# Single-unit places for the side work in the second and the last batch of a selective scan

## The reference, cut to what matters

```python
x = einsum('ed,bld->bel', in_proj_w, hidden)            # DI = 512 channels
u = silu(conv4(x) + conv_b)
x_dbl = einsum('ke,bel->bkl', x_proj_w, u)               # dt_lo (16), B (16), C (16)
delta = softplus(dt_proj_w @ dt_lo + dt_proj_b)
state = state * exp(delta * A) + (delta * u) * B         # over 512 steps, 16 states n
y = sum_n state * C + D * u
x = x + tanh(g_x) * (y * silu(layernorm(x)))
x = x + tanh(g_f) * moe(layernorm(x))                    # top 6 of 16 experts and a shared one
```

## Time and profile before

| what | us |
|---|---|
| three runs, median | 1437.23 (1434.22 to 1439.29) |
| profiled execution, its own time | 1440.73 |
| its span in the trace | 1438.6 |
| batch 0, first scan to first scan of batch 1 | 46.3 to 159.2 |
| batch 1 (second) | 159.2 to 273.4, 114.2 |
| batch 2 (third) | 273.4 to 385.1, 111.7 |
| batch 3 (last) | 385.1 to 488.2, 103.1 |
| last product of POOL in the scans | ends at 491.67 |
| experts | from 492.4 to the end |

### The profile page before, as it was taken

One profiled execution on the slowest core, in us unless ns is written; L12 is line 12 of the kernel. 1 busy time (PEld: TensorE's weight loads), 2 busy tenths in 40 slices (PEclk: granted clock), 3 DMA queues, 4 the chain that ended last, 5 costly groups with the idle time before them and its releaser, 6 DMA issues.

```text
span 1438.6 us, 32257 instructions
## 1 busy us (share of the span) xinstructions
PE 1355.8 (94%) x8480; PEld 1212.9 (84%) x8481; DVE 786.1 (55%) x1362; ACT 730.9 (51%) x1317; POOL 952.3 (66%) x673
## 2 busy tenths in 40 slices
PE   7897998998898899999999999999999999999996
PEld 2686887887888799999998989989889888898895
DVE  5878898898999854653333333333333333333331
ACT  5898897898889464343332333323333233333321
POOL 0588899998998847887455665556645666646631
PEclk8899999998999999999999999999999999999998
DMA  4121123222242365645455435555445544455332
GB/s 137 38 68 37 53 67 96 67 85 79 75 157 68 124 130 105 143 83 140 83 143 144 130 64 142 143 144 135 113 84 141 144 131 108 97 137 138 75 60 36
DMA packets 65042, 149.13 MB, mean 104 GB/s; under 512 B 16976, under 2 KB 17616, under 8 KB 62656
## 3 DMA queue, kind: packets, MB, share of 16 engines
q0 software_dynamic: 31024, 62.10, 22.7%
q1 hardware_dynamic: 33392, 81.21, 17.2%
q10 hardware_dynamic: 560, 4.98, 1.0%
HBM read 101.50 MB, written 48.99 MB: 105 GB/s over the span
## 4 chain that ended last, share of the span: by engine, by line
PE 65%; ACT 2%; DVE 2%; issue 1%; POOL 0%; DVEq 0%; POOLq 0%; ACTq 0%
PE bank L1706 20%; PE bank L1686 19%; PE bank L1687 18%; PE bank L1674 3%; PE bank L1697 3%; DVE hs L1168 1%; PE bank L1591 1%; ACT dA L784 1%; PE bank L1577 1%; PE bank L1589 0%; ACT gt L799 0%; POOL hc L945 0%; DVE xl L1359 0%; DVE du L1182 0%; ACT bdiag L802 0%
## 5 line engine op out<-in xcount | busy, mean ns | idle before, releaser
L945 POOL TENSOR_TENSOR hc<-hs,crow 128x512 f32<-128x512 f32 x256 | 325.0, 1304 | 91.7 <-DVE hs L1168 86.2
L1686 PE MATMUL bank<-w,xh 128*128 (+1 forms) x1088 | 368.9, 340 | 8.1 <-issue 4.7
L1011 POOL DMA_INDIRECT out_x<-ys,aid x104 | 170.7, 1641 | 277.0 <-issue 218.8
L1687 PE MATMUL bank<-w,xh 128*128 (+1 forms) x1088 | 351.0, 323 | 0.0
L1168 DVE TENSOR_TENSOR_SCAN hs<-dA,bank 128x512 f32<-128x512 f32 x256 | 295.8, 1208 | 48.5 <-PE bank L1591 31.8
L1706 PE MATMUL bank<-w,ah 128*128 (+1 forms) x816 | 266.0, 407 | 2.7 <-DVE al L1395 2.7
L1395 DVE TENSOR_TENSOR al<-bank,ah 128x384 fp32r<-128x384 f32 x136 | 75.9, 558 | 331.6 <-ACT ah L860 280.4
L1686 PEld LDWEIGHTS bank<-w,xh 128*128 128x128 f32 x1088 | 204.3, 188 | 37.8 <-issue 34.8
L1687 PEld LDWEIGHTS bank<-w,xh 128*128 128x128 f32 x1088 | 206.3, 190 | 2.2
L866 ACT COPY ys<-bank 128x512 f32<-128x512 f32 x136 | 79.9, 587 | 196.7 <-PE bank L1706 189.0
L1687 PE MATMUL bank<-w,xl 128*128 (+1 forms) x544 | 175.8, 323 | 0.0
(11 more groups left out here) (183 smaller groups left out, 2056.6 us busy)
## 6 DMA issues: line engine op xcount, KB each, us to landing
wraw<-in_wall SPq DMA_DIRECT2D x16, 2176.0 KB
crow<-c_rows SPq DMA_DIRECT2D x64, 256.0 KB, 3.3
xt<-token_rows_turned SPq DMA_DIRECT2D x32, 256.0 KB
out_x<-ys POOLq DMA_DIRECT2D x32, 256.0 KB
wraw<-in_wall ACTq DMA_DIRECT2D x2, 2176.0 KB
token_rows<-rowb SPq DMA_DIRECT2D x4, 1028.0 KB
xrow<-in_x SPq DMA_DIRECT2D x4, 1024.0 KB, 8.0
out_x<-xrow SPq DMA_DIRECT2D x4, 1024.0 KB, 4.9
```

The lines of the kernel that those rows point to most:

```text
L945: nc.gpsimd.tensor_tensor(hc[:, j, :], hs[:, j, :], crow[:, n % 4, :], ALU.mult).then_inc(hc_done, 1)
L1011: pool.indirect_dma_start(out_rows, bass.IndirectOffsetOnAxis(ap=aid[:, s:s + 1], axis=0), ys[:, s, :], None, bounds_check=TOKENS - 1, oob ...
L1686: nc.tensor.matmul(gate_bank[:, 0:I], xx, columns(w, off + ww + k * 2 * I, I), start=first, stop=last)
L1687: mm = nc.tensor.matmul(up_bank[:, 0:I], xx, columns(w, off + ww + k * 2 * I + I, I), start=first, stop=last)
```

## The change

It changes tables only: every piece stays on its engine and in its batch, and the same set of pieces is done. In batch 1 and batch 3 they now stand behind other units, mostly singly; the tables of batches 0 and 2 are as before. Two entries change their order within ACT's list: in batch 1 `table` now stands before `silu` and `siluz`, and in batch 3 `siluz` stands behind unit 40 and `table` behind unit 45. SP's pieces (loads and stores) of these batches move too, and POOL's `low` pieces of the last batch.

```diff
-PE_SECOND = {3: [("xproj", "pre", 0), ("xproj2", "pre", 0)], 7: [("dt", "pre", 0), ("dt", "pre", 1)], 11: [("dt", "pre", 2)], 15: [("dt", "pre", 3)],
-             23: [("bt", "pre", 0)], 27: [("inproj", "next", 0)], 35: [("xlt", "epi", 0), ("inproj", "next", 1), ("xlt", "epi", 1)],
-             39: [("inproj", "next", 2), ("xlt", "epi", 2)], 43: [("inproj", "next", 3)], 47: [("xlt", "epi", 3)],
-             51: [("gate", "epi", 0), ("dut", "pre", 0), ("gate2", "epi", 0), ("dut", "pre", 1)], 55: [("szt", "own", 0), ("dut", "pre", 2)],
-             59: [("szt", "own", 1), ("szt", "own", 2), ("dut", "pre", 3), ("szt", "own", 3)]}
+PE_SECOND = {3: [("xproj", "pre", 0), ("xproj2", "pre", 0)], 8: [("dt", "pre", 0)], 9: [("dt", "pre", 1)], 14: [("dt", "pre", 2)],
+             17: [("dt", "pre", 3)], 25: [("bt", "pre", 0)], 27: [("inproj", "next", 0)],
+             35: [("xlt", "epi", 0), ("inproj", "next", 1), ("inproj", "next", 2)], 36: [("xlt", "epi", 1)], 40: [("xlt", "epi", 2)],
+             43: [("inproj", "next", 3)], 47: [("xlt", "epi", 3)], 51: [("gate", "epi", 0), ("gate2", "epi", 0), ("dut", "pre", 0)],
+             53: [("dut", "pre", 1)], 55: [("szt", "own", 0), ("dut", "pre", 2)], 59: [("szt", "own", 1)], 60: [("szt", "own", 2)],
+             61: [("szt", "own", 3), ("dut", "pre", 3)]}
...
-ACT_SECOND = {11: [("xproj", "pre", 0)], 15: [("decay", "pre", 0)], 19: [("decay", "pre", 1)], 23: [("decay", "pre", 2), ("softplus", "pre", 0)],
...
-              43: [("xlt", "epi", 1), ("inproj", "next", 2)], 47: [("inproj", "next", 3), ("xlt", "epi", 2)],
-              51: [("xlt", "epi", 3), ("silu", "next", 0), ("siluz", "own", 0), ("table", "own", 0)], 55: [("dut", "pre", 0), ("dut", "pre", 1)],
-              59: [("dut", "pre", 2), ("szt", "own", 0)],
-              63: [("szt", "own", 1), ("szt", "own", 2), ("szt", "own", 3), ("dut", "pre", 3), ("gate", "epi", 0)]}
...
+              33: [("softplus", "pre", 2)], 35: [("softplus", "pre", 3), ("rstd", "both", 0)], 36: [("norm", "epi", 0)],
+              39: [("xlt", "epi", 0), ("inproj", "next", 1)], 40: [("inproj", "next", 2)], 41: [("xlt", "epi", 1)], 47: [("xlt", "epi", 2)],
+              49: [("inproj", "next", 3)], 52: [("xlt", "epi", 3), ("table", "own", 0), ("silu", "next", 0), ("siluz", "own", 0)],
+              55: [("dut", "pre", 0)], 58: [("dut", "pre", 1)], 59: [("gate", "epi", 0)], 62: [("szt", "own", 0), ("dut", "pre", 2), ("szt", "own", 1)],
+              63: [("szt", "own", 2), ("szt", "own", 3), ("dut", "pre", 3)]}
...
-ACT_LAST = {19: [("rstd", "both", 0)], 23: [("norm", "epi", 0)], 26: [("high", "last", 0)], 27: [("xlt", "epi", 0), ("xlt", "epi", 1)],
-            28: [("high", "last", 1)], 30: [("high", "last", 2)], 32: [("high", "last", 3)], 34: [("high", "last", 4)], 36: [("high", "last", 5)],
-            38: [("high", "last", 6)], 39: [("xlt", "epi", 2), ("xlt", "epi", 3)], 40: [("high", "last", 7)],
-            43: [("siluz", "own", 0), ("table", "own", 0), ("szt", "own", 0)], 47: [("szt", "own", 1)], 55: [("szt", "own", 2)],
-            59: [("szt", "own", 3), ("gate", "epi", 0)]}
+ACT_LAST = {22: [("rstd", "both", 0), ("norm", "epi", 0)], 24: [("high", "last", 0), ("high", "last", 1)], 27: [("xlt", "epi", 0)],
+            29: [("xlt", "epi", 1)], 30: [("high", "last", 2)], 34: [("high", "last", 3)], 35: [("high", "last", 4)], 38: [("high", "last", 5)],
+            39: [("high", "last", 6), ("xlt", "epi", 2), ("xlt", "epi", 3)], 40: [("siluz", "own", 0)], 42: [("szt", "own", 0)],
+            45: [("szt", "own", 1), ("table", "own", 0)], 47: [("high", "last", 7)], 57: [("gate", "epi", 0)], 58: [("szt", "own", 2)],
+            61: [("szt", "own", 3)]}
...
+DVE_SECOND = {3: [("y", "epi", 0)], 12: [("x2", "epi", 0)], 15: [("excess", "pre", 0)], 17: [("x2", "epi", 1), ("excess", "pre", 1)],
+              25: [("x2", "epi", 2)], 26: [("x2", "epi", 3)], 27: [("stats2", "epi", 0)], 31: [("inproj", "next", 0), ("nmr", "both", 0)],
+              35: [("delta", "pre", 0), ("inproj", "next", 1)], 37: [("excess", "pre", 2), ("inproj", "next", 2)], 41: [("delta", "pre", 1)],
+              48: [("excess", "pre", 3)], 49: [("inproj", "next", 3)], 51: [("gate", "epi", 0), ("delta", "pre", 2)], 54: [("delta", "pre", 3)],
...
-DVE_LAST = {3: [("y", "epi", 0)], 7: [("x2", "epi", 0)], 11: [("x2", "epi", 1)],
-            15: [("x2", "epi", 2), ("x2", "epi", 3), ("stats2", "epi", 0), ("nmr", "both", 0)], 35: [("gate", "late", 1), ("gate", "late", 2)],
-            43: [("gate", "late", 3), ("gate", "late", 4), ("gate", "epi", 0)]}
+DVE_LAST = {3: [("y", "epi", 0)], 8: [("x2", "epi", 0)], 9: [("x2", "epi", 1)], 11: [("x2", "epi", 2)], 13: [("x2", "epi", 3)],
+            14: [("stats2", "epi", 0)], 17: [("nmr", "both", 0)], 37: [("gate", "late", 1)], 39: [("gate", "late", 2)], 44: [("gate", "late", 3)],
+            46: [("gate", "late", 4)], 48: [("gate", "epi", 0)]}
...
-POOL_LAST = {3: [("x2", "epi", 0)], 7: [("x2", "epi", 1)], 11: [("x2", "epi", 2), ("x2", "epi", 3)], 33: [("low", "last", 0)], 36: [("low", "last", 1)],
-             39: [("low", "last", 2)], 42: [("low", "last", 3)], 45: [("low", "last", 4)], 48: [("low", "last", 5)], 51: [("low", "last", 6)],
-             54: [("low", "last", 7)]}
+POOL_LAST = {3: [("x2", "epi", 0)], 4: [("x2", "epi", 1)], 6: [("x2", "epi", 2), ("x2", "epi", 3)], 22: [("low", "last", 0)],
+             33: [("low", "last", 1), ("low", "last", 2)], 43: [("low", "last", 3), ("low", "last", 4), ("low", "last", 5)],
+             61: [("low", "last", 6), ("low", "last", 7)]}
...
-SP_SECOND = {0: [("load", "next", 0)], 8: [("xproj", "pre", 0)], 12: [("x2", "epi", 0)], 28: [("rows", "epi", 0), ("xrow", "pre", 0)], 55: [("turned",
-             "epi", 0)]}
+SP_SECOND = {8: [("load", "next", 0)], 21: [("xproj", "pre", 0)], 41: [("x2", "epi", 0)], 53: [("xrow", "pre", 0)], 55: [("turned", "epi", 0)],
+             57: [("rows", "epi", 0)]}
...
-SP_LAST = {12: [("x2", "epi", 0)], 24: [("rows", "epi", 0)], 36: [("weights", "late", 0)], 43: [("turned", "epi", 0)]}
+SP_LAST = {10: [("rows", "epi", 0)], 31: [("x2", "epi", 0)], 43: [("turned", "epi", 0)], 61: [("weights", "late", 0)]}
```

## The result

| | before | after |
|---|---|---|
| median (lowest to highest), us | 1437.6 (1434.2 to 1439.3) | 1445.9 (1445.6 to 1447.1) |
| ratio to before, 95% interval | 1 | 1.0051 [1.0038, 1.0064] |
| span of the profiled execution | 1438.6 | 1443.5 |
| table loads on ACT | 18 | 30 |

A forecast was written before the change was run, and what follows sets the result against it. Each batch of scans was taken as one chain over five engines, none full, with 10 us of waits per changed batch. Batch 1 -2.6, batch 2 +10.8, batch 3 -2.5 sum to +5.7 on 1437.2: 1443 us, range 1431 to 1451.

The forecast's parts named there:

- The Ln's table without Exp: Batch 2: the table a Ln loads has no Exp, so each Exp behind it loads again, 1.28 us a load.
- the Exp's table without Ln: Batch 2: an Exp's table lacks Ln, so softplus 0 to 3 and rstd take two loads each, 10 in all.
- up to nmr 5.9 forecast: Batch 2: DVE waits 1.0 at unit 24 and 4.9 at nmr for late rstd, a shift of 5.9 us.
- 2.3 for a slow clock of PE: Batch 2 behind nmr: PE idles some 4 us, its granted clock falls, and DVE waits for it, 2.3 us lost.
- At the gate 2.6 forecast: Batch 2 behind units 43 and 47: loads at dA 44 and softplus 3 lengthen the chain to PE's gate by 2.6 us.
- The gain of 1.3 behind unit 27: Batch 1: with inproj 0 behind 31, DVE's two waits after PE ran dry go but for 0.1, gain 1.3 us.
- The 1.2 of small waits up to unit 51: Batch 1: half of the smaller waits up to unit 51, 2.1 us together, go, gain 1.2 us.
- The loss of 3.0 at `dut` 2: Batch 1 behind unit 55: PE's dut 2 waits for ACT to read out dut 1's bank, loss 3.0 us.
- The chooser's long wait: Batch 3 behind unit 44: DVE's chooser may wait for POOL's products and three low, up to 8 us in hand.
- Rival 1: Batch 2: the joint table returns by itself at dA 53, two loads instead of twelve, only gains left: 1432 us; chance 0.08.
- Rival 3: Batches 1 and 3: gains eaten by dut 2, late xrow and the chooser, both come out even: 1450 us; chance 0.20.
- Rival 2: Placement better than counted: batch 1 gains 8, batch 3 gains 5, against +9 in batch 2: 1436 us; chance 0.20.

The follow-up runs named there:

- e1: The kernel before with one edit: joint table load put ahead of Silu behind unit 51 of batch 1; 1448.2 us, ratio 1.0061 to before.
- e2: The changed kernel with the joint table put back right behind Silu and siluz in batch 1, behind siluz in batch 3; 1435.5 us, ratio 0.9972 to before.
- e5: The changed kernel with one more hand-written joint table load behind unit 0 of batch 2; 1435.6 us, ratio 0.9984 to before.
- e6: e1 with batch 2's nmr behind DVE's unit 31 instead of 27 and norm behind ACT's 35 instead of 31; 1450.2 us, ratio 1.0084 to before.
- e4: The kernel before with only batch 1's pieces placed as changed, the table still behind Silu and siluz; 1436.7 us, ratio 0.9991 to before.
- e9: e2 with batch 1's inproj 2 of DVE back behind 39, inproj 3 of DVE and ACT behind 47; 1432.6 us, ratio 0.9967 to before; repeated, 1433.2.
- e8: e2 with POOL's eight low products placed one at a time, behind units 22 to 52; 1435.9 us, ratio 0.9977 to before.

## Why the prediction was right, and where not

**The sign and the size held.** 1443 was forecast, 1445.9 measured, with 1437.6 for before: +5.7 forecast, +7.3 by the ratio. The mechanism was the one named: 12 loads, on the lines named, batch 2 paying for a list entry of batch 1. e1, e2 and e5 show it from three sides (+8.8, -11.4, -9.6 us). That the sum lies so near is in part luck: batch 1 gave 3.3 less than forecast by the windows, batch 2 cost 1.2 less, batch 3 gave 0.4 more, and the two spans differ by another 2.5 outside these batches, which was not forecast.

**Batch 2, +10.8, measured +9.65 (e1: 9.1).** The Ln's table without Exp was taken from one pair of rows in the experts, and was right; the Exp's table without Ln was chosen between two bounds, and was right too. The Trainium skill (ScalarE: Activation LUTs, Table sets: the hidden batching unit) has one load for a Ln and the Exp behind it. The trace has one for each, unless the joint table was brought by hand. Its price of a load with the drain (same page, What ACT_TABLE_LOAD costs) isn't seen either: from 249.08 to the next activation at 250.38 are 1.30 us, and eleven such loads cost 8.8 us of time in e1, less than their own length. By terms: up to nmr 5.9 forecast, 6.2 measured. Behind it 2.3 for a slow clock of PE, and there the lag fell by 0.6 up to unit 43: no lag came of that term, though the clock did fall. At the gate 2.6 forecast, 4.0 measured. These errors cancel in part, and e6 shows why the ledger was of the wrong kind: local waits were added up where one engine was full. The ten loads less ACT's idle time up to the gate, 12.8 - 5.5, give 7.3 in one step, a lower bound of the 9.6 measured there. The prediction had read the sign of this, ACT busy for 19.94 of 20 us, and used it only up to nmr.

**Batch 1, -2.6, measured +0.7, with the loads back -1.3 us of time (e4).** These are the terms that failed, though the total is uncertain: windows of the same code differ by 2 us, and the interval of e4 reaches from 0 to -2.4. The waits are the firmer evidence: DVE was idle for 15.5 us of the batch before (114.20 - 98.75) and for 17.1 now (114.90 - 97.82). The gain of 1.3 behind unit 27 did not come: inproj 0 behind 31 stands right beside nmr and PE stops there all the same, 2.96 at 211.28 where it had 2.06 before. The 1.2 of small waits up to unit 51 (half of the 2.1 named would be 1.05) did not come either: there is a stop of PE of 2.44, and DVE waits 1.24 and 1.59, the latter much as the 1.60 before unit 44 in the kernel before. The wait of 2.61 at unit 52 was to vanish; what vanished there came back one piece earlier, 3.43 at the gate, and 1.11 behind it. The loss of 3.0 at `dut` 2 did not come at all (PE's du behind unit 55 follows without a wait), so the errors partly cancel again. e9 moved two of the pieces back, and does not settle it: PE's stop shrank by 0.4, and the length of the batch came out either way.

**Batch 3, -2.5, measured -2.9** to the point where the experts start, by another road. The wait for rstd of 3.70 went as said, but of the 4.4 and 2.9 us counted on from it at scans 24 and 32 only 1.9 and 1.6 came, from the first scan of the batch. The chooser's long wait was forecast behind unit 44, beside three `low`, and there eq took 0.73; it was sc behind 37 that took 5.47. The prediction's term runs to the end of POOL's last product and has the two `low` behind unit 61 in it, so the 1.5 us between the end of the scans and that product are inside it. That the experts "are not touched" held for their time: from POOL's first product behind the scans to the end are 944.3 us before and 943.9 now. It overlooked that the load of the next weights, and ACT's cast behind it, wait for the last `low`, 8.30 us here. That wait cost nothing by itself: DVE's `xl` behind the cast ends 0.55 after POOL's last product in both kernels.

**Ends of the range.** Rival 1 (1432) fell at the first softplus of batch 2. Rival 3 (1450) had the right feature, gains eaten, in batch 1 only. Rival 2 (1436) had the places worth 8 + 5; e2 has 4.

## What to carry to other kernels

An engine's hidden state belongs to the order of its queue: when pieces are moved, look at who restores the state and whether that still comes behind whoever destroys it, also one batch on, in code that did not change. Where an engine is full, price what is added to it by its whole length up to the next point at which another engine has to meet it, less its idle time up to there (a lower bound: 7.3 of 9.6 here), and don't add up single waits, since taking one away may only move it. Follow each moved piece to whoever waits for it, past the end of the loop in which it moves, and ask what else the next step waits for. And before a window of one stage is taken as a gain or a loss, compare it between profiles of the same code.

## What the runs showed of the hardware

A small product on DVE that reads two tiles of SBUF can stand until POOL has run out of ready products, and not only to the end of the one in progress. sc, 128x64, took 0.22 to 0.23 us among the experts, where POOL had nothing in hand, and 3.54 to 5.50 in the last batch of all thirteen profiles, where it ended 0.08 to 0.09 after the end of POOL's run each time; here in the changed kernel:

```profile
447.72 5.47 DVE L1223 TENSOR_TENSOR sc<-ex,rsm 128x64 f32<-128x64 f32 x1
448.16 4.95 POOL L946 TENSOR_TENSOR hc<-hs,crow 128x512 f32<-128x512 f32 x4
...
454.53 2.50 POOL L946 TENSOR_TENSOR hc<-hs,crow 128x512 f32<-128x512 f32 x2 [1.42 <-DVE hs L1169]
```

It need not. In batch 2 the same sc took 0.24 to 1.29 and ended 0.08 to 0.09 after the one product in progress in all thirteen profiles, while POOL ran on with three more. In the changed kernel it ended at 334.97, the product at 334.89, in the middle of this run:

```profile
331.14 4.98 POOL L946 TENSOR_TENSOR hc<-hs,crow 128x512 f32<-128x512 f32 x4 [0.56 <-DVE hs L1169]
```

What decides between the two is open. DVE's scans, which take at most one input from SBUF, ran beside the same products at 1.2 us each. The Trainium skill (SBUF — State Buffer, SBUF: two separate sides) says that such a DVE operation and a GpSimd one that reads SBUF exclude each other for one whole instruction. The trace agrees on who excludes whom and, in batch 2, on how long; in the last batch it differs: two to four products behind the one in progress went ahead, in e8 one of them a `low`. What it costs is bounded by POOL's backlog, and as DVE feeds POOL, the gap of 1.42 behind it is POOL's. That moving such a step to a unit at which POOL has nothing in hand would give some of it back was not tried.
